# Mamba layer of an eight-layer kernel: sums two steps behind, products of delta and x inside the scan, closing norms of layer 5 interleaved

## What is computed

```python
x_act = silu(causal_conv4(x @ in_proj_x) + conv_b)
delta = softplus(x_act @ dt_proj_w.T + dt_proj_b)
B, C  = split(x_act @ x_proj_w.T)
h_n   = exp(delta * A_n) * h_n + (delta * x_act) * B_n     # over time, one n of 16
y     = sum_n h_n * C_n + x_act * D
out   = (y * silu(z)) @ out_proj_w.T
```

## Time and profile before

| | us |
|---|---|
| three runs: median (lowest, highest) | 1105.49 (1100.1, 1108.96) |
| the profiled execution, device time | 1111.02 |
| its span in the trace | 1109.2 |
| VectorE busy in the span | 823.3 |
| PE busy in the span | 932.4 |

### The profile page before, as it was taken

The page is one execution under the profiler, slowest core; times in us unless marked ns, Lnnn a source line. Parts: engine busy times, 40 slices in busy tenths (PEclk is TensorE's granted clock), DMA queues, the critical chain, the costliest instruction groups (busy, mean ns, idle before and its releaser), DMA issues.

```text
span 1109.2 us, 11145 instructions
## 1 busy us (share of the span) xinstructions
PE 932.4 (84%) x2933; PEld 543.2 (49%) x2933; DVE 823.3 (74%) x1167; ACT 611.0 (55%) x1115; POOL 669.4 (60%) x465
## 2 busy tenths in 40 slices
PE   6869977588889967899999999987577777797997
PEld 3324432233337635688888888632122323234775
DVE  4995435999975568666666666587999999975754
ACT  5756675400356654555565555576555455535556
POOL 3030123698862133577777777519999989962773
PEclk9979988699999977899999999999799899988999
DMA  2000120000020004367666666301333222224251
GB/s 81 1 0 1 43 83 17 0 0 1 0 63 9 0 24 105 93 146 155 142 148 156 145 142 156 85 0 43 86 86 86 78 74 77 75 67 99 69 148 39
DMA packets 29929, 78.25 MB, mean 71 GB/s; under 512 B 3968, under 2 KB 13824, under 8 KB 25696
## 3 DMA queue, kind: packets, MB, share of 16 engines
q1 hardware_dynamic: 29888, 77.78, 28.0%
HBM read 75.93 MB, written 1.84 MB: 70 GB/s over the span
## 4 chain that ended last, share of the span: by engine, by line
PE 37%; DVE 14%; ACT 4%; issue 3%; POOL 0%; DVEq 0%; ACTq 0%
PE ps L619 37%; DVE g L3160 5%; DVE y L3160 4%; DVE tmp L2464 1%; ACT ps L1427 1%; ACT sq L1427 1%; DVE g L2464 1%; DVE rstd L2464 1%; ACT rstd L1427 1%; DVE ps L2464 1%; DVE normed L2464 0%; ACT g L1427 0%; DVE g L3135 0%; ACT parts L1427 0%; DVE g L3119 0%
## 5 line engine op out<-in xcount | busy, mean ns | idle before, releaser
L619 PE MATMUL ps<-parts 128*128 128x512 f32 x1704 | 417.5, 404 | 16.1 <-DVE g L2464 4.9
L619 PEld LDWEIGHTS ps<-parts 128*128 128x128 f32 x1704 | 322.7, 190 | 105.5 <-issue 18.8
L619 PE MATMUL ps<-g,arena 128*128 128x512 f32 (+2 forms) x408 | 194.7, 618 | 26.6 <-POOL g L2348 15.1
L1427 ACT ACTIVATE g<-ps 128x512 f32<-128x512 f32 (+1 forms) x216 | 127.5, 597 | 153.9 <-PE ps L619 147.7
L2464 DVE TENSOR_TENSOR ps<-g,ps 128x512 f32<-128x512 f32 x160 | 111.3, 696 | 95.8 <-PE ps L619 74.4
L2299 POOL TENSOR_TENSOR parts<-g,parts 128x512 fp32r<-128x512 f32 x112 | 144.5, 1290 | 59.8 <-ACT parts L1427 56.9
L619 PEld LDWEIGHTS ps<-g,arena 128*128 128x128 f32 (+1 forms) x408 | 77.9, 199 | 134.3 <-issue 89.9
L1427 ACT ACTIVATE ps<-g,small 128x512 f32<-128x512 f32 x131 | 89.2, 687 | 87.9 <-DVE y L3160 42.8
L1427 ACT ACTIVATE parts<-g 128x512 fp32r<-128x512 f32 (+3 forms) x243 | 125.8, 546 | 21.0 <-DVE g L2464 13.9
L2421 POOL TENSOR_TENSOR g<-g,arena 128x1024 f32<-128x1024 f32 x48 | 113.4, 2390 | 0.1
L2464 DVE TENSOR_TENSOR g<-ps,g 128x512 f32<-128x512 f32 (+1 forms) x140 | 98.9, 707 | 17.9 <-DVE ps L2464 3.3
(11 more groups left out here) (226 smaller groups left out, 1201.5 us busy)
## 6 DMA issues: line engine op xcount, KB each, us to landing
g<-coef_scratch SPq DMA_DIRECT2D x56, 512.0 KB, 6.2
arena<-b_scratch SPq DMA_DIRECT2D x48, 256.0 KB, 3.3
g<-in_moe_dram SPq DMA_DIRECT2D x34, 192.0 KB, 4.7
g<-coef_scratch SPq DMA_DIRECT2D x24, 256.0 KB, 5.3
arena<-coef_scratch SPq DMA_DIRECT2D x24, 256.0 KB, 4.2
g<-b_scratch SPq DMA_DIRECT2D x16, 256.0 KB, 3.2
g<-in_rope_dram SPq DMA_DIRECT2D x1, 2048.0 KB, 8.8
g<-in_moe_dram SPq DMA_DIRECT2D x2, 768.0 KB, 7.5
```

What stands on the lines that cost most here:

```text
L619: return nc.tensor.matmul(o, lhsT, rhs, start=start, stop=stop, **kw)
L1427: return nc.scalar.activation(o, i, func, **kw)
```

## The change

PE's loop now sums a step that POOL multiplied three iterations later, as before, and a step that VectorE multiplied two iterations later. The product of delta and x leaves deltas() and becomes delta_times_x(c): chunk 0 behind deltas(1), chunks 1 to 3 in VectorE's loop at k = 2, 6 and 10, ahead of scan(k + 1). At the end of layer 5, PE's var5("post", 0) and var5("post", 1) go between the last two centrings and the last down_product; ACT does y_copy5(0) and y_copy5(1) ahead of the last hidden_hi, and root5("post", 0) ahead of y_copy5(3). PE's wait for the weights of layer 6 now stands behind those two averages.

```diff
--- before.py
+++ after.py
@@ -1187,9 +1187,15 @@
                     for k in (0, 1):
                         round_of(2 * i + (2 * begun + r0 + 2 + k), 1 - k, (k,))
                 round_of(r0 + pairs, 1, (0,), True)
-                for c in range(1, CHUNKS):
-                    down_product(4 * (r0 + pairs) + c, c, 1, False, True)
-                    centre5(c - 1)
+                down_product(4 * (r0 + pairs) + 1, 1, 1, False, True)
+                centre5(0)
+                down_product(4 * (r0 + pairs) + 2, 2, 1, False, True)
+                centre5(1)
+                down_product(4 * (r0 + pairs) + 3, 3, 1, False, True)
+                var5("post", 0)
+                centre5(2)
+                var5("post", 1)
+                centre5(3)
 
             def centre5(c):
                 pe.wait_ge(s["y_ready"], y_before(5) + c + 1)
@@ -1209,10 +1215,7 @@
                     mm(ps[:, 4 * i + c, :], W(6, "wx", i * 128, i * 128 + 128), H(c)).then_inc(s["xs_bank"], 1)
 
             experts(5, 64, 32, 0, 0)
-            centre5(CHUNKS - 1)
             pe.wait_ge(s["w_loaded"], 7 * 16)
-            var5("post", 0)
-            var5("post", 1)
             var5("post", 2)
             var5("pre", 0)
             var5("post", 3)
@@ -1319,10 +1322,11 @@
             pe.wait_ge(s["w_loaded"], 16 * LAYERS)
             for step in range(STEPS):
                 c, n = step // 16 - 1, step % 16
-                if 3 <= step < STEPS - 1:
+                if step - 3 in BY_POOL:
                     sum_n(step - 3)
+                if step >= 2 and step - 2 not in BY_POOL:
+                    sum_n(step - 2)
                 if step == STEPS - 2:
-                    sum_n(step - 2)
                     sum_n(step - 1)
                 if c >= 0 and step < STEPS:
                     if n == 3:
@@ -1928,6 +1932,8 @@
                     round_of(2 * i + (2 * begun + r0 + 3), 0, 16 * i + 16 * (begun + base1 + 3))
                 round_of(r0 + pairs, 1)
                 use_log_exp()
+                y_copy5(0)
+                y_copy5(1)
                 hidden_hi(4 * (r0 + pairs) + 3, 3)
 
             def y_copy5(c):
@@ -1948,13 +1954,11 @@
                 f(rstd[:, cols(c)], rstd[:, cols(c)], ACT.Exp, scale=-0.5).then_inc(s["rstd_ready"], 1)
 
             experts(5, 64, 32, 0, 0)
-            y_copy5(0)
-            y_copy5(1)
             square5(0)
             y_copy5(2)
             square5(1)
+            root5("post", 0)
             y_copy5(3)
-            root5("post", 0)
             square5(2)
             root5("post", 1)
             square5(3)
@@ -3134,6 +3138,8 @@
                     dve.wait_ge(s["dt_ready"], 2 * c + 2 - i)
                     v.scalar_tensor_tensor(G(4 + i, c), ps[:, 4 * i + c, :], W(6, "dt_b", i, i + 1), G(8 + i, c),
                                            ALU.add, ALU.max).then_inc(s["dl_ready"], 1)
+
+            def delta_times_x(c):
                 dve.wait_ge(s["dl_ready"], 2 * c + 2)
                 tt(g[:, 6:8, cols(c)], g[:, 4:6, cols(c)], g[:, 0:2, cols(c)]).then_inc(s["du_ready"], 1)
 
@@ -3142,6 +3148,7 @@
             deltas(0)
             clip_dt(2)
             deltas(1)
+            delta_times_x(0)
             clip_dt(3)
             deltas(2)
             deltas(3)
@@ -3215,6 +3222,8 @@
                         h_back7(c)
                     if n == 14 and c < 2:
                         clip7(c)
+                if k in (2, 6, 10):
+                    delta_times_x(k // 4 + 1)
                 if k + 1 < STEPS:
                     scan(k + 1)
                 if k not in BY_POOL:
```

## The result

The changed kernel is slower: 1137.99 us median (1136.01 to 1140.98, four runs) against 1106.96 for the kernel before (1100.1 to 1108.96, four runs, one more than in the table above), a ratio of 1.0291 with the 95% interval 1.0264 to 1.0318. The forecast was 1123.5 us in a range that ended at 1133: the sign and the mechanism were right, the size was little more than half of the measured one. The profiled execution has a span of 1136.8 us, 27.6 more than before.

What follows compares the result with a forecast made beforehand. VectorE was taken to bound the scan, with PE's bursts becoming tight. Terms -1.6 (layer 5) + 3.8 (products) + 8.3 (bursts) + 7.5 (clock) = +18.0 us gave 1123.5 us on the median 1105.5; range 1106 to 1133.

Steps and rivals of the forecast that it cites:

- Where the limit is: Scan stage: VectorE is its limit, so whatever is added to it or makes it wait is added to the end.
- The bursts at full clock, +8.3: PE's double sums in the scan delay VectorE: 3.9 at n = 10, 4.1 at n = 13, 0.3 at the gate.
- the plain places: Scan iterations such as n = 4 and 7: spread_c behind two sums still comes 0.5 us ahead of VectorE's need.
- The clock, +7.5 (bounds 0 and 16): Scan: longer PE idle times lower its clock, slowing the sums after them; 9.0 us less 1.5 already paid at clip7.
- The nine places that the working counted: n = 10, n = 13 and gate, three times each: no slack after a long PE idle time, 9 x 1.5 x 4/6 = 9.0 us.
- the upper bound: Clock term in the scan at most 16 us: all nine places pay 1.5 and four at n = 7 pay 1.0, less 1.5.
- The four in six: Scan before the change: after four of six PE idle times of 1.97 to 2.33 us the clock fell; used as the share paying.
- the rival in which the clock holds: Scan: double sums cost time but PE's clock stays up; +9.0 or so, 1114.5 us, chance 0.20.
- Products of delta and x, +3.8: Three products moved into the scan: 1.8 us won ahead of it, 5.6 paid on VectorE inside it.
- Layer 5, -1.6: End of layer 5: first root 2.3 us earlier, h_back6 and layer 6's first products about 1.5 earlier; bounds 0 and 2.3.
- The end of the scan, 0: VectorE's last product waits 4.32 us for PE; the new order moves step 59's sum but removes none, so no change.

Runs made afterwards that it cites:

- the filled kernel: Kernel before with only PE's new sum order, plus zero-matrix products in PE's iterations without a sum and ahead of the gate's sum: 1119.03 us against 1105.44, ratio 1.0115.
- the new order alone: Kernel before with only PE's new order of sums, without the layer 5 edits or moved products: 1137.42 us against 1107.37, ratio 1.0304.
- the combined kernel: Kernel before with layer 5 changed, average and router product ahead of sums, step 58 summed earlier, delta products in VectorE's waits: 1101.69 us against 1105.43, ratio 0.9958.

## Why the prediction was too low

Its steps, one by one:

- **Where the limit is**: right. VectorE is the limit of the scan, and each us that it waited or worked more is in the 34.56.
- **The bursts at full clock, +8.3**: right place by place, and 8.8 by the stage of the filled kernel against the stage before; by the times that kernel costs 13.6 us, so the term may be some us low. The places: 1.14 at n = 10 where the working had 1.3; 3.21 at the router where it had 3.4; 0.28 at n = 13 of chunk 0 where it had 0.4; nothing at the gates where it had 0.1; and the 0.5 us of slack in the plain places. At n = 10 of chunk 0 it had nothing, since delta_times_x(3) gives room; the kernel after waits 0.35 there, the one without moved products 1.67.
- **The clock, +7.5 (bounds 0 and 16)**: this is the step that failed; it measured 20.4 us in the stage with the sums alone. Place by place, the waits of the new order alone less those of the filled kernel are 19.7 us at thirteen places. The nine places that the working counted, at 9 x 1.5 x 4/6 = 9.0, cost 15.2: eight of them paid, not six, and 1.9 us each, not 1.5, three of them over 2.5, as a slow double sum loses 2.3 us (5.92 against 3.60) and not the 1.5 of a single one. Five places that the working put at nothing cost another 4.5: n = 4, 7 and 10 of chunk 0 and two at the start of chunk 1. Those with 0.5 us of slack (n = 4 and n = 7) were kept for the upper bound, though the working itself had the idle time ahead of them at over 3 us. The four in six was taken from idle times of 2.0 to 2.3 us and used for ones of 2.0 to 5.4, most of them near 3. The trace of the kernel before had one idle time of 2.70 us, and the sum behind it was slow, which the working left out:

```profile
789.68 0.61 PE L619 MATMUL ps<-g,sel 96*128 96x512 bf16 x1 [2.70 <-DVE rstd L2464]
790.08 3.20 PE L619 MATMUL ps<-tmp,const 128*128 128x512 f32 x4
```

- **A slip in the sum**: the slow sum ahead of the router in the kernel before was taken off twice, once in the bursts (3.4 less the 2.3 that it waited with the slow sum, 1.1) and once as the 1.5 in the clock's term. Without it the clock's term is 9.0 and the sum +19.5, and the rival in which the clock holds 1116.0 instead of 1114.5. The upper bound of the clock has the same slip and the same 1.5 for each place.
- **The rule that was set aside**: the prediction had beside it the rule of the Trainium skill (TensorE: Matmul & The Clock Gate, HAM oscillation) that work in bursts with waits between pays for the lower clock in every burst. In the traces of the new order it was not every burst, some came at full clock after idle times of 2.2 to 3.6 us (2.23 at 923.97, 3.57 at 948.54), but 28% of the stage was at the lower level and eight of the nine places paid; the rule was nearer than four in six.
- **Products of delta and x, +3.8**: right in size, +3.3 us by the times of the kernel with this part alone; 2.5 us won ahead of the scan (1.8 taken, 2.6 the bound), 6.0 to 6.3 paid in it (5.6 taken). Where the working had the first scan wait for POOL, it waited for ACT's decay.
- **Layer 5, -1.6**: right side, -2.35 in the trace, at the end of its bounds, and -3.0 by the times; the collision of h_back6 with POOL's square that was kept in mind (1.40 us for 0.69) did not occur any more on VectorE; of POOL's squares two took 1.42 us for 1.04, one before.
- **The end of the scan, 0**: nearly. The last product with C waited 2.43 instead of 4.32, but the one before it 1.98 that it had not: the same backlog, reached at another point.

With 20.4 for the clock in place of 7.5 the sum would have been -1.6 + 3.8 + 8.3 + 20.4 = +30.9, against +31.0 between the medians. That it comes so close is in part luck, as the terms for layer 5 and for the bursts are off by 1.4 and up to 5.3 us by the times, in opposite directions. The parts by their measured times alone are -3.0 + 3.3 + 30.1 = +30.4.

## What to carry to other kernels

When the same work is regrouped on an engine that others wait for, write down for each burst when its result is due and how long the engine idles ahead of it; the sum of the work says nothing. On TensorE a long idle time ahead of a burst is to be priced at the lower clock at every place where the burst has no slack of its own, the places with a little slack included, and by the length of the new burst. Where a few idle us recur, cheap products in them can win time without any reordering: some 17 of the 30 us lost in the kernel with the bad order, 3 us in the kernel before, and nothing in the combined kernel, whose VectorE had no wait for PE left inside the scan.

## What the runs showed of the hardware that was not expected

- More work made the engine's results come sooner: adding 0.86 us products with zeros to PE's idle time raised its granted clock from 0.86 to 1.00 over 190 us and took 16.5 us off the kernel (each kernel against the kernel before in its own runs).
- The same VectorE product of two SBUF tiles, 128 x 1024, took 1.20 us at one place (at k = 30 of the combined kernel), 1.43 to 2.65 at others inside the scan, and 3.09 ahead of the scan. At the place with 1.20 POOL stood idle when the product began, and POOL's own product, begun 0.32 us later, took 3.10 us instead of 2.35: there POOL paid. At the place with 3.09 POOL had begun a product 0.34 us earlier. The Trainium skill (SBUF — State Buffer, Who interferes with whom) makes it an exclusive lock, so that one has to wait for the whole instruction of the other. An estimate by that rule from the rows here is 2.35 - 0.34 + 1.20 = 3.2 us, and 3.6 as the worst case; the 3.09 nearly agrees. The mean of 2.1 inside the scan lies between 1.2 and 3.6, as it would if the products meet POOL's at any point.

```profile
871.22 1.20 DVE L2471 TENSOR_TENSOR g<-g 128x1024 f32<-128x1024 f32 x1
...
871.54 3.10 POOL L2437 TENSOR_TENSOR tmp<-g,sq 128x1024 f32<-128x1024 f32 x1 [0.62 <-ACT sq L1434]
...
769.31 7.94 POOL L2428 TENSOR_TENSOR g<-g,arena 128x1024 f32<-128x1024 f32 x3
```
